# The border tiles' six steps moved from the end to the front of each edge aggregation

## What is computed

```python
Wh = (h @ W).reshape(N, HEADS, OUT_CH)               # 6250 x 4 x 64
e  = leaky_relu(s[row] + d[col])                     # one score for each edge and head
e  = exp(e - max(e))
e_sum = segment_sum(e, row)
h_new = segment_sum(Wh[col] * (e / e_sum[row]), row)
```

## Time and profile before

| | us |
|---|---|
| median of 3 runs | 6546.49 (6545.6 to 6547.97) |
| profiled execution, own time | 6551.56 |
| its span | 6549.7 |
| POOL, gathers L881, busy | 3076.2 (of 3477.7) |
| PE busy | 4884.5 (75%) |
| DVE busy | 4362.4 (67%) |
| ACT busy | 1839.7 (28%) |

### The profile page before, as it was taken

One profiled execution on the slowest core, in us unless ns is written; L12 is line 12 of the kernel. 1 busy time (PEld: TensorE's weight loads), 2 busy tenths in 40 slices (PEclk: granted clock), 3 DMA queues, 4 the chain that ended last, 5 costly groups with the idle time before them and its releaser, 6 DMA issues. The chain is left out here.

```text
span 6549.7 us, 91189 instructions
## 1 busy us (share of the span) xinstructions
PE 4884.5 (75%) x22060; PEld 3588.0 (55%) x22061; DVE 4362.4 (67%) x8849; ACT 1839.7 (28%) x5179; POOL 3477.7 (53%) x3669
## 2 busy tenths in 40 slices
PE   1456777777677763699867777767778768999999
PEld 1445555555555552499544454445555546666665
DVE  8987887888788878733666666666776666333333
ACT  8322322232223322244410000012222216333332
POOL 0117777777777775155157777777777743000000
PEclk8668888888888886799988888887777778999999
DMA  1012222222222222322555555555555543000001
GB/s 60 17 47 57 57 56 57 58 57 57 57 57 58 57 56 61 113 71 70 158 145 139 138 140 140 138 143 146 147 149 148 147 113 72 5 5 10 5 5 39
DMA packets 383777, 532.65 MB, mean 81 GB/s; under 512 B 123389, under 2 KB 244242, under 8 KB 383506
## 3 DMA queue, kind: packets, MB, share of 16 engines
q0 software_dynamic: 139648, 299.92, 19.1%
q1 hardware_dynamic: 243986, 231.21, 11.7%
HBM read 473.88 MB, written 56.96 MB: 81 GB/s over the span
## 5 line engine op out<-in xcount | busy, mean ns | idle before, releaser
L881 POOL DMA_INDIRECT got<-table,st_idx x3232 | 3076.2, 952 | 1010.1 <-issue 905.2
L959 PE MATMUL ps_sum<-weighted,hot 128*128 128x260 f32 x6464 | 1848.3, 444 | 184.4 <-DVE acc L1031 179.7
L959 PEld LDWEIGHTS ps_sum<-weighted,hot 128*128 128x128 f32 x6464 | 1380.2, 224 | 601.0 <-DVE acc L1031 277.0
L1031 DVE TENSOR_TENSOR acc<-acc,ps_sum 128x260 f32 x1664 | 706.8, 425 | 734.5 <-PE ps_sum L959 597.9
L944 PE MATMUL ps_score<-score_split,hot_t 128*128 x3232 | 246.2, 184 | 985.6 <-DVE z L1011 960.8
L1023 DVE TENSOR_TENSOR weighted<-got,ps_weight 128x2048 f32<-128x2048 f32 x404 | 921.5, 2281 | 7.6 <-issue 4.9
L944 PEld LDWEIGHTS ps_score<-score_split,hot_t 128*128 128x128 bf16 x3232 | 191.6, 100 | 1167.2 <-issue 1149.7
L916 ACT ACTIVATE ps_weight<-z 128x32 f32<-128x32 f32 x404 | 81.2, 201 | 2664.9 <-DVE z L1011 2664.9
L3080 DVE SCALAR_TENSOR_TENSOR x_res<-ps_yf,comb,x_res 128x256 f32 x392 | 189.6, 484 | 637.5 <-PE ps_yf L2979 637.5
L982 DVE TENSOR_TENSOR hot<-ps_score,row_loc 128x1024 f32<-128x1024 f32 x404 | 492.0, 1218 | 3.5
L2959 PE MATMUL ps_hf<-acc,ws_f 128*128 (+2 forms) x896 | 348.6, 542 | 1.6 <-ACTq L3006 1.6
(11 more groups left out here) (531 smaller groups left out, 7341.7 us busy)
## 6 DMA issues: line engine op xcount, KB each, us to landing
spread<-row_list SPq DMA_DIRECT2D x404, 256.0 KB
got<-table,st_idx POOLq DMA_INDIRECT x3232, 2.8
gate_xin<-ball_rows SPq DMA_DIRECT2D x98, 128.0 KB, 2.2
got_y_e<-y_rows SPq DMA_DIRECT2D x10, 896.0 KB
table<-row_e SPq DMA_DIRECT2D x50, 130.0 KB, 3.1
ball_rows<-xt SPq DMA_DIRECT2D x10, 640.0 KB, 4.7
mix_xin<-ball_rows SPq DMA_DIRECT2D x49, 128.0 KB, 2.0
xn_rows<-xs_m SPq DMA_DIRECT2D x49, 128.0 KB, 1.7
```

What stands on the lines that cost most here:

```text
L881: pool.indirect_dma_start(got[:, r, k, :], None, table, bass.IndirectOffsetOnAxis(ap=st_idx[:, r, k:k + 1], axis=0))\
L959: last = nc.tensor.matmul(ps_g[:, p % 2, 0:AW], hot[:, r % 2, k, :], weighted[:, r % 2, k, :], start=(k == n * p), stop=(k == n * p + n - 1))
L1031: nc.vector.tensor_tensor(acc[:, ds(b * AW, AW)], acc[:, ds(b * AW, AW)], ps_g[:, p % 2, 0:AW], ALU.add).then_inc(added, 1)
```

## The change

The six steps of border tiles become steps 0 to 5 (turn 0 and the first half of turn 1), and the 196 pair steps come behind them. The entries, the tiles, `col_idx`, `row_loc` and `row_list` are laid out in that order, so a pair step's first entry is now i × 4 + 24. Since the border tiles are listed last in the sort (they need a fetch through PE), the row list that holds them, list 0, is turned, cast and sent last (`LIST_ORDER`). The copy of the block numbers is made in two pieces. One more turn of `GateMix` is written out, since turn 1 now holds border steps.

```diff
--- before.py
+++ after.py
@@ -29,11 +29,12 @@
 PAIR_STEPS = -(-EJ // KT)
 PAIRS = PAIR_STEPS * KT // 2
 SINGLES = NT - 1
-STEPS = PAIR_STEPS + SINGLES // KT
+SINGLE_STEPS = SINGLES // KT
+STEPS = PAIR_STEPS + SINGLE_STEPS
 ENTRIES = PAIRS + SINGLES
 TILES = STEPS * KT
 SORTED = -(-EJ // P) * P
-assert SINGLES % KT == 0 and PAIR_STEPS % STEP_RING == 0
+assert SINGLES % KT == 0 and PAIR_STEPS % STEP_RING == 0 and STEP_RING < SINGLE_STEPS <= 2 * STEP_RING
 D = 256
 NTP = NT + NT % 2
 NPAD = NTP * P
@@ -150,6 +151,7 @@
 LAST_KEY = KEY_BASE | ((64 * P - 1) << COL_BITS)
 GROUPS = SORTED // P
 LISTS = ((0, 4), (4, 8), (8, 12), (12, 13))
+LIST_ORDER = (1, 2, 3, 0)
 LOW_G = 8
 assert SORTED - P < TILES <= SORTED and N <= 64 * P and NPAD <= 1 << COL_BITS
 
@@ -490,8 +492,9 @@
                 sp.dma_start(dsts[0:ER, EC:EJ], dst[EC * P:E].rearrange("(p j) -> p j", j=1)).then_inc(loaded, 16)
                 guest.load(sp, x)
                 guest.spill(sp)
-                for c, (g0, g1) in enumerate(LISTS):
-                    sp.wait_ge(list_kept, c + 1)
+                for n, c in enumerate(LIST_ORDER):
+                    g0, g1 = LISTS[c]
+                    sp.wait_ge(list_kept, n + 1)
                     rows = min(P, TILES - g0 * P)
                     sp.dma_start(g.row_list.rearrange("i (k n) -> (i k) n", n=P)[g0 * P:min(g1 * P, TILES), :].rearrange("(q p) n -> p q n", p=rows),
                                  rows_t[0:rows, g0:g1, :]).then_inc(list_out, 16)
@@ -547,9 +550,10 @@
                     act.wait_ge(key_turned, c + 1)
                     to = turned_keys[0][:, g0 * P:g1 * P] if g1 <= 12 else turned_keys[1]
                     nc.scalar.copy(to, ps[:, c, 0:(g1 - g0) * P]).then_inc(key_kept, 1)
-                for c, (g0, g1) in enumerate(LISTS):
+                for n, c in enumerate(LIST_ORDER):
+                    g0, g1 = LISTS[c]
                     rows = min(P, TILES - g0 * P)
-                    act.wait_ge(list_turned, c + 1)
+                    act.wait_ge(list_turned, n + 1)
                     nc.scalar.copy(rows_t[0:rows, g0:g1, :], ps[0:rows, c, 0:(g1 - g0) * P].rearrange("p (q n) -> p q n", n=P)).then_inc(list_kept, 1)
 
             @block.tensor
@@ -595,8 +599,9 @@
                             of = turned_keys[0][:, q * P:(q + 1) * P] if q < 12 else turned_keys[1]
                             last = nc.tensor.matmul(ps_t[:, 0:SINGLES], of, tile_hot[:, q, :], start=(q == 0), stop=(q == GROUPS - 1))
                 last.then_inc(fetched, 1)
-                for c, (g0, g1) in enumerate(LISTS):
-                    pe.wait_ge(listed, 1 if g1 * P <= 2 * PAIRS else 2)
+                for c in LIST_ORDER:
+                    g0, g1 = LISTS[c]
+                    pe.wait_ge(listed, 1 if g0 * P >= SINGLES else 2)
                     for q in range(g0, g1):
                         n = min(P, TILES - q * P)
                         last = nc.tensor.transpose(ps[0:n, c, (q - g0) * P:(q - g0 + 1) * P], g.row_loc[:, q * P:q * P + n], g.ident[:, :])
@@ -685,7 +690,8 @@
                         dve.wait_ge(blocks_of, 1)
                         link(nc.vector.tensor_scalar(block_of[:, 0:PAIRS].rearrange("p (c n) -> p c n", c=2), ps_b[:, :, 0:PAIRS // 2],
                                                      float(NT - 1), None, ALU.min))
-                        link(nc.vector.tensor_copy(g.pair_block[:, :], block_of[0:1, :]))
+                        nc.vector.tensor_copy(g.pair_block[:, SINGLES:ENTRIES], block_of[0:1, 0:PAIRS])
+                        link(nc.vector.tensor_copy(g.pair_block[:, 0:SINGLES], block_of[0:1, PAIRS:ENTRIES]))
                         link(nc.vector.tensor_scalar(block_of[:, :], block_of[:, :], float(-P), None, ALU.mult))
 
                 def list_edges(lo, hi, key, part, down):
@@ -763,12 +769,12 @@
                 assert now[0] == now[1] and 2 * len(steps) == guest.LAST_SLOT
                 link(nc.vector.tensor_scalar(own_pad[:, :], g.lane[:, :], float(NT * P), None, ALU.add))
                 of, other = keys[now[0]], keys[1 - now[0]]
-                list_edges(0, 2 * PAIRS, of[:, 0:2 * PAIRS], other[:, 0:2 * PAIRS], block_of[:, 0:PAIRS])
+                list_edges(SINGLES, TILES, of[:, 0:2 * PAIRS], other[:, 0:2 * PAIRS], block_of[:, 0:PAIRS])
                 dve.sem_inc(listed, 1)
                 guest.moments(dve)
                 dve.wait_ge(fetched, 1)
                 link(nc.vector.tensor_copy(of[:, 2 * PAIRS:TILES], ps_t[:, 0:SINGLES]))
-                list_edges(2 * PAIRS, TILES, of[:, 2 * PAIRS:TILES], other[:, 2 * PAIRS:TILES], None)
+                list_edges(0, SINGLES, of[:, 2 * PAIRS:TILES], other[:, 2 * PAIRS:TILES], None)
                 dve.sem_inc(listed, 1)
 
 
@@ -839,13 +845,13 @@
 
         def entries(i):
 
-            return KT // 2 if not isinstance(i, int) or i < PAIR_STEPS else KT
+            return KT // 2 if not isinstance(i, int) or i >= SINGLE_STEPS else KT
 
         def first_entry(i):
 
-            if not isinstance(i, int) or i < PAIR_STEPS:
-                return i * (KT // 2)
-            return PAIRS + (i - PAIR_STEPS) * KT
+            if not isinstance(i, int) or i >= SINGLE_STEPS:
+                return i * (KT // 2) + SINGLE_STEPS * (KT // 2)
+            return i * KT
 
         def low(i):
             return range(entries(i) // 2)
@@ -2402,7 +2408,7 @@
     KV_TURNS = NTP // 2
     OUT_AT = KV_TURNS
     END = 2 * KV_TURNS
-    spans = ((1, OUT_AT - 1, "keys"), (OUT_AT - 1, OUT_AT, "last keys"),
+    spans = ((1, 2, "keys"), (2, OUT_AT - 1, "keys"), (OUT_AT - 1, OUT_AT, "last keys"),
              (OUT_AT, OUT_AT + 1, "first out"), (OUT_AT + 1, OUT_AT + 2, "first out"), (OUT_AT + 2, END - 2, "out"),
              (END - 2, END - 1, "out"), (END - 1, END, "out"))
```

## The result

The changed kernel takes **6513.6 us** (median of 5 runs, 6510.15 to 6518.7) against 6546.49 before: a ratio of 0.9948, 95% interval 0.9935 to 0.9962, some 33 us. The forecast was 6516 and 30.2 us less. The profiled execution has a span of 6516.8 us against 6549.7.

What follows compares the result with a forecast made beforehand. POOL's gathers bound both passes, so only the stretch after each pass's last gather could move. Gains of 13.3 (pass 0) and 17.6 (pass 1) less 0.7 (sort) gave 30.2 us: 6516 us at the median, range 6501 to 6531.

Steps and rivals of the forecast that it cites:

- my sign of being wrong: POOL's gathers end later, measured from each pass's first one, or pass 1's end stays over 35 us behind.
- End of pass 0: Last add 12.5 us after the last gather instead of 25.8: a gain of 13.3 us, bounds 10.8 to 15.0.
- The lag: Time from the end of a step's last gather to the start of its scale; 3.5 us forecast ending pass 0.
- the tail: Last scale's start to a pass's last add: six adds, 9.0 us forecast, between 7.3 (fast) and 11.5 (throttled).
- End of pass 1: End lag 22.8 us instead of 40.4, from scale lag 13.8 plus 9.0: a gain of 17.6, bounds 2 to 29.6.
- say +6: Lag in pass 1 from one added register operation per step in DVE's list, 96 steps without slack; bounds nothing to +14.
- The front: Border steps starting each pass cost 0: the lag reaches 27 us, under the 28.0 that POOL's four-buffer ring hides.
- The sort: At the sort's end, the last list has four tiles: three more PE transposes, wider cast; +0.7 us, bounds 0 to 1.5.
- A: Pass 1's lag is not worked off and stays near 20 us or grows; 6522, at worst 6532; chance 0.27.
- B: Dear border steps at the front fill the ring; POOL stands for 26 us, about 6542; chance 0.06.
- C: Front at half clock, 20 us per border step: POOL stands 83 us and 6516 becomes 6599; chance 0.03.
- D: Only the six adds at each pass's end are saved: 4 us a pass, 6539; chance 0.04.

Runs made afterwards that it cites:

- the eight in the experiment: The change plus eight more 40 ns register operations in DVE's list in each looped step of pass 1, ahead of the first low add: ratio 0.9971, median 6529.9 us.
- heavier front: The change plus five clearings of 128 x 448 numbers in DVE's list in each of the six border steps of both passes: ratio 0.9972 to the kernel before.
- eight operations cost nothing on PE: The change plus eight more register operations in PE's list in each looped step of pass 1, ahead of the first low sum: ratio 0.9947 to the kernel before.

## Why the prediction was right, and where it was not

- **What bounds it.** Right: what moved was the stretch behind POOL's gathers. By the letter of my sign of being wrong they did end later, 2.0 and 1.8 us after 2036 and 2024. No gather waited longer for a scale than the usual 0.30 us, so it isn't the front's stall. In pass 0 the gathers of kernels with the same front took 2035.0 to 2041.7 us, so 2.0 is spread; in pass 1 every kernel with the border steps in front has 2026.1 or more, and the one with them last 2023.5, so 1.8 seems to belong to the new order. Its cause is open.
- **End of pass 0.** 11.6 us against 12.5 forecast, gain 14.1 against 13.3. The lag was 4.5 instead of 3.5, the tail 7.1 instead of 9.0. The tail was mis-sized by the clock: I took 0.80 from the end before, where PE was not fed "without a pause" as I wrote but busy for 20.80 of 26 us, and the new tail was granted 1.00. By the Trainium skill's rule ("TensorE: Matmul & The Clock Gate", Part 1) it would have been the throttled tail, as I read it. The traces speak against that: of the 17 tails of six adds, twelve were granted 1.00 and took 7.1 us (my fast price was 7.3), three 0.78 with 7.3 to 7.7 us, and two 0.64 with 9.5. None was at 0.50.
- **End of pass 1.** 18.5 us against 22.8, gain 21.9 against 17.6. The fall over the last six steps was 17.4 − 11.5 = 5.9 against 6, but such a near hit is luck: in the other kernels that end with pair steps it was 2.8 to 5.6. The tail was again 7.1 instead of 9.0. The term that failed is the register operation, "say +6": of the eight in the experiment only 1.2 to 1.9 us each came through, since it stands ahead of a wait for PE's sum. I had looked at the wait for gathers, which was gone, and taken that for no slack at all. The lag of step 195 was +3.6 in this run; other runs of the same DVE loop give from −5.6 (heavier front) to +1.9, and the loop without the operation −1.2 and +5.6, so that one operation can't be seen in it.
- **The front.** Right, at a cost of 0: peaks of 19.5 and 23.2 us, bound 27, against a limit of 28 which the heavier front shows to be real.
- **The sort.** Right: +0.63 against +0.7; pass 0 began 1.6 us later in this profile, of which the sort's own spread is a part.
- **The sum.** That 30.2 us were forecast and 32.9 measured between the spans is partly luck: the ends gave 36.0 against 30.9, the start of pass 0 cost 1.6 and not 0.7, and the sum had no term for the 3.8 us of the gathers and the 2.3 that the other stages gave back.
- **Rivals.** A, that the lag stays: the front's lag was worked off in the first half of pass 1, to 4 us; it grew again in the second, as A said, but fell to 11.5 and ended at 18.5, not 29. B and C, a stalled front: they need the heavier front to come about, and then cost 12 to 16 us. D, six adds only: no, the scale lags fell by 10.2 and 17.9 us.
- **What stays open** is how far the lag of pass 1's second half goes with the clock. It varied from 8 to 19 us at step 195 in runs whose aggregation differs little there, and the stretch's granted clock from 0.77 to 0.79. 8.2, 13.8 and 15.7 us stood beside 0.79 and 17.4 beside 0.77, but 12.6 and 19.4 both beside 0.78, and no run held the clock fixed. Open too is why eight operations cost nothing on PE: its list may be read ahead, or DVE may set the pace.

The kernel without the added register operation is not measurably faster than the change.

## What to carry to other kernels

A pipeline that falls behind in its heavy steps needs light ones after them: put the heavy steps where slack follows, and compare their lag with the depth of the ring that lets the feeder run on. Before pricing an added operation at its full length, look at every wait behind it on its engine, not only at the one that has run out. And look at the work behind the last transfer of a stage apart from the rest, since no transfer is left to hide it.

## What was not expected of the hardware

The same six adds behind the last scale took 7.1 us at a granted clock of 1.00, 7.3 to 7.7 at 0.78 and 9.5 at 0.64, and which of them a run got varied at the end of pass 0 between kernels whose pass 0 is the same but for small edits; at the end of pass 1 all eight tails of six adds were granted 1.00. And a front of border steps ran at 0.65 to 0.76 of the clock in pass 0 (three stretches of 20 us from 500 to 560 us, by the view of busy time by stretch), where pair steps had 0.83 to 0.91 before.
